# The 17 remaining contraction rows of the first MLP layer: one bf16 product over slots of split values in place of an f32 product

## The reference

```
ada = silu(c) @ W_ada + b_ada
shift_msa, scale_msa, gate_msa, shift_mlp, scale_mlp, gate_mlp = split(ada, 6)
h = layernorm(x) * (1.0 + scale_msa) + shift_msa
x = x + gate_msa * attention(h, W_qkv, b_qkv, W_proj, b_proj)
h = layernorm(x) * (1.0 + scale_mlp) + shift_mlp          # 128 x 144 per sequence
mlp = gelu(h @ W_fc1 + b_fc1, approximate=True) @ W_fc2 + b_fc2   # W_fc1 is 144 x 576
x = x + gate_mlp * mlp
# then: U = qr(P), R = expm(A(silu(cond) @ W.T + b))
x_rot = x + (z @ R - z) @ U.T,   z = x @ U                 # z is 128 x 64
```

## Time and profile before

| what | value |
|---|---|
| median of 3 runs | 407.22 us (405.56 to 407.91) |
| span of the profiled execution (first to last instruction) | 404.8 us |
| PE busy | 370.0 us, 91% |
| DVE, ACT, POOL busy | 254.6, 195.5, 134.7 us |
| chain that ended last, by engine | PE 79%, DVE 9%, ACT 4%, issue 4% |
| L1283 and L1284 | 160 instructions each, 33.3 and 30.9 us busy |
| mean granted TensorE clock | 0.959 |

### The profile page before, as it was taken

How to read it: one execution, slowest core, us unless ns; L and a number is a source line. 1 busy time by engine, 2 the same in 40 slices (tenths; PEclk the granted TensorE clock), 3 DMA queues, 4 the chain that set the end, 5 groups by cost and what they waited for, 6 DMA issues and landing times.

```text
span 404.8 us, 13218 instructions
## 1 busy us (share of the span) xinstructions
PE 370.0 (91%) x4399; PEld 289.4 (71%) x4399; DVE 254.6 (63%) x1056; ACT 195.5 (48%) x432; POOL 134.7 (33%) x400
## 2 busy tenths in 40 slices
PE   0699898889999999999999999998799999999995
PEld 0553686658777777777777777787578878787783
DVE  7560064888788789789789778968824332333233
ACT  1314444466577568568667666854233222212220
POOL 4431051543553554455455455433331000000000
PEclk9989566899999999999999999999999999999998
DMA  8515000000000000000000000000000000000000
GB/s 224 166 33 204 2 2 2 1 2 4 1 2 0 0 0 0 0 0 0 0 0 0 0 2 3 2 2 2 2 4 2 2 15 13 11 15 15 15 8 29
DMA packets 8517, 7.93 MB, mean 20 GB/s; under 512 B 1054, under 2 KB 8065, under 8 KB 8356
## 3 DMA queue, kind: packets, MB, share of 16 engines
q1 hardware_dynamic: 7776, 6.67, 5.6%
q10 hardware_dynamic: 708, 0.83, 0.7%
HBM read 6.29 MB, written 1.20 MB: 19 GB/s over the span
## 4 chain that ended last, share of the span: by engine, by line
PE 79%; DVE 9%; issue 4%; ACT 4%; DMA 1%; POOL 1%; ACTq 1%; DVEq 0%; POOLq 0%
PE bank L1283 6%; PE bank L1284 4%; PE bank L1127 4%; PE bank L1111 4%; PE bank L1145 4%; PE bank L1135 4%; PE bank L1291 4%; PE bank L1082 4%; PE bank L1100 3%; PE bank L1071 3%; PE bank L1049 3%; PE bank L1090 3%; PE bank L1072 3%; PE bank L1101 3%; PE bank L1046 2%
## 5 line engine op out<-in xcount | busy, mean ns | idle before, releaser
L423 POOL TENSOR_TENSOR root<-rec,mhalf 128x1 f32 (+1 forms) x64 | 34.6, 541 | 108.7 <-DVE Z L807 107.7
L866 DVE TENSOR_REDUCE nmax<-bank 128x4 f32<-128x512 f32 x64 | 43.2, 674 | 43.6 <-PE bank L1090 42.4
L587 ACT ACTIVATE E<-bank 128x512 f32<-128x512 f32 x64 | 38.0, 594 | 24.4 <-PE bank L1101 24.0
L609 ACT ACTIVATE gT<-bank 128x512 f32<-128x512 f32 x16 | 9.6, 597 | 65.7 <-PE bank L1284 65.7
L593 ACT ACTIVATE QT<-bank 128x512 bf16<-128x512 bf16 x32 | 19.0, 595 | 40.7 <-PE bank L1082 40.7
L597 ACT ACTIVATE KT<-bank 64x512 bf16<-64x512 bf16 x64 | 37.5, 587 | 0.8
L1100 PE MATMUL bank<-QT,KT 128*128 128x128 bf16 x256 | 36.3, 222 | 0.0
L1101 PE MATMUL bank<-NMT,headsel 128*128 128x128 bf16 x256 | 35.8, 220 | 0.0
L1135 PE MATMUL bank<-Z,sel 128*128 128x128 f32 x128 | 29.0, 310 | 6.1 <-DVE Z L813 6.1
L1283 PE MATMUL bank<-hT,wfc1a 128*128 128x128 f32 (+1 forms) x160 | 33.3, 290 | 0.0
L1100 PEld LDWEIGHTS bank<-QT,KT 128*128 128x128 bf16 x256 | 24.1, 98 | 9.7 <-issue 9.7
(11 more groups left out here) (231 smaller groups left out, 926.6 us busy)
## 6 DMA issues: line engine op xcount, KB each, us to landing
gates<-gates_dram SPq DMA_DIRECT2D x1, 2304.0 KB, 8.6
x_all<-in_x_dram SPq DMA_DIRECT2D x4, 288.0 KB, 7.5
out_dram<-x_all SPq DMA_DIRECT2D x16, 72.0 KB, 1.6
wskew<-in_L_cond_W_dram SPq DMA_DIRECT2D x4, 283.5 KB
wada<-in_L_cond_W_ada_dram ACTq DMA_DIRECT2D x1, 432.0 KB
wfc1a<-in_L_cond_W_fc_dram SPq DMA_DIRECT2D x1, 288.0 KB
wfc2a<-in_L_cond_W_fc_dram SPq DMA_DIRECT2D x1, 288.0 KB
wproj<-in_L_cond_W_proj_dram SPq DMA_DIRECT2D x16, 5.1 KB
```

What stands on the lines that cost most here:

```text
L423: link(nc.gpsimd.tensor_tensor(root[:, at], rec[:, at], mhalf[:, 0:1], ALU.pow))
L587: nc.scalar.activation(E[:, q, :, :].rearrange("p i t -> p (i t)"), bank[4][:, :], ACT.Exp).then_inc(s_E, 1)
L866: nc.vector.tensor_reduce(nmax[:, q % 2, 4 * (q // 2):4 * (q // 2) + 4], bank[3][:, :].rearrange("p (i m) -> p i m", i=4), AX.X, ALU.max, ...
```

## The change

The second product of each chunk is done in bf16, with all parts of the f32 values. Eight slots of 16 rows make up the 128 contraction rows. The 16 remaining rows of W_fc1 are loaded into six slots of `wfc1r`, three copies of the bias into three rows of a seventh. On DVE they are turned once into `wfc1b` (bf16), in which a slot holds the first, second or third bf16 part of the weights. The tokens' 16 remaining channels are spread over the eight slots by normalizing a broadcast of them (`xr`), and transposed. ACT modulates them twice, into `hR` (f32) and `hB` (bf16), with `mod2r`, the scale and shift spread over the slots by one product in the prologue. Then `parted` on DVE replaces the slots from row 64 on by the second part and those from row 96 on by the third. The sum over the slots is the sum of six of the nine products of parts.

```diff
         def _(sp):
             sp.wait_ge(k_pad, 2)
-            sp.dma_start(wfc1b[0:C2, :], W_fc1[C1:C, :]).then_inc(s_ldm, 16)
-            sp.dma_start(wfc1b[C2:K2, :], b_fc1.rearrange("(a n) -> a n", a=1)).then_inc(s_ldm, 16)
+            for n in WHOLE:
+                sp.dma_start(wfc1r[C2 * n:C2 * n + C2, :], W_fc1[C1:C, :]).then_inc(s_ldr, 16)
+            for n in range(3):
+                sp.dma_start(wfc1r[ONES + n:ONES + n + 1, :], b_fc1.rearrange("(a n) -> a n", a=1)).then_inc(s_ldr, 16)
...
+            def modulated_again(b):                                   # ACT, in place of modulated
+                wait(act, m_xnT, b + 1)
+                wait(act, m_fc1, b)
+                for t, m, o, row in ((hR, mod2r, 128, 0), (hB, mod2r, 128, 0), (hT1, mod1, 0, 2)):
+                    nc.scalar.activation(t[:, :], bank[0][:, o:o + 128], ACT.Identity, bias=m[:, row, bass.ds(b, 1)],
+                                         scale=m[:, row + 1, bass.ds(b, 1)]).then_inc(m_hT, 1)
...
             dve.wait_ge(k_id, N_ID)                                   # DVE, prologue, ahead of the wait for s_Gp
+            nc.vector.tensor_copy(rep[:, :, :], ident[0:C2, 0:C2]...to_broadcast([C2, 8, C2])).then_inc(s_rep, 1)
+            ...                                                       # five tensor_reduce and three small ones: slots
             dve.sem_inc(k_more, 1)
+            dve.wait_ge(s_rep, 9)
+            dve.wait_ge(s_ldr, 16 * 9)
+            nc.vector.tensor_copy(wfc1b[:, :], wfc1r[:, :]).then_inc(s_wB, 1)
+            STT(wfc1d[:, :], wfc1b[:, :], slots[:, 5:6], wfc1r[:, :], ALU.mult, ALU.add).then_inc(s_wB, 1)
+            nc.vector.tensor_copy(wfc1b[:, :], wfc1d[:, :]).then_inc(s_wB, 1)
+            STT(wfc1b[:, :], wfc1b[:, :], slots[:, 6:7], wfc1d[:, :], ALU.mult, ALU.add).then_inc(s_wB, 1)
+            dve.wait_ge(s_repP, 1)
+            TS(mod2r[:, 0, :], bank[6][:, 416:416 + B], ...)           # and one more for mod2r[:, 1, :]
...
+            def normalized_again(b):                                  # DVE, in place of normalized
+                TS(xn[:, 0:C1], xb[:, 0:C1], mean, rstd[:, bass.ds(b, 1)], ALU.subtract, ALU.mult).then_inc(m_xn, 1)
+                TS(xr[:, :, :], x_all[:, bass.ds(b, 1), C1:C].to_broadcast([128, 8, C2]), mean, ...).then_inc(m_xn, 1)
+
+            def parted(b):
+                wait(dve, m_hT, 3 * b + 2)
+                two, three = slice(64, 128), slice(96, 128)
+                link(TT(hD[two, :], hR[two, :], hB[two, :], ALU.subtract))
+                link(nc.vector.tensor_copy(hB[two, :], hD[two, :]))
+                TT(hB[three, :], hD[three, :], hB[three, :], ALU.subtract).then_inc(m_hB, 1)
...
             def mlp(b, parity):                                       # DVE, behind the add of b-3, ahead of xT1
+                if within(b, -1, B - 2):
+                    parted(b + 1)
...
+            def transposed_again(b):                                  # PE, in place of transposed
+                pe.transpose(bank[0][:, 128:256], xr[:, :, :]..., ident[:, :])
+                pe.transpose(bank[0][:, 0:128], xn[:, 0:C1], ident[:, :]).then_inc(m_xnT, 1)
...
-            generator_entries(0, 3)                                   # PE, prologue
+            generator_entries(0, 1)
+            pe.wait_ge(s_mod, 4)
+            pe.wait_ge(s_gsb, 1)
+            pe.wait_ge(s_rep, 1)
+            mm(bank[6][:, 416:416 + 2 * B], rep..., mod2[:, 2:4, :]..., start=True, stop=True).then_inc(s_repP, 1)
+            generator_entries(1, 3)
...
             def fc1(b):
-                wait(pe, m_hT, 2 * b + 2)
+                wait(pe, m_hT, 3 * b + 3)
                 for k in range(FK + 1):
                     mm(dst, wfc1a[:, 128 * k:128 * k + n], hT1[:, :], start=True, stop=False)
-                    ins = mm(dst, wfc1b[:, 128 * k:128 * k + n], hT2[:, :], start=False, stop=True)
+                    if k == 0:
+                        wait(pe, m_hB, b + 1)
+                    ins = mm(dst, wfc1b[:, 128 * k:128 * k + n], hB[:, :], start=False, stop=True)
```

More of the change, by code:

```diff
@@ L106, in adaln_block_then_rotation @@
         wqkv1, wqkv2 = sb("wqkv1", [C1, 3 * C]), sb("wqkv2", [128, 3 * C])
-        wfc1a, wfc1b = sb("wfc1a", [C1, FF]), sb("wfc1b", [128, FF])
+        wfc1a, wfc1b = sb("wfc1a", [C1, FF]), sb("wfc1b", [128, FF], BF16)
+        wfc1r, wfc1d = sb("wfc1r", [128, FF]), sb("wfc1d", [128, FF])
         wfc2a, wfc2b = sb("wfc2a", [128, FK, C]), sb("wfc2b", [FR + 1, C])
@@ L143, in adaln_block_then_rotation @@
         hT1, hT2 = sb("hT1", [C1, 128]), sb("hT2", [128, 128])
+        xr, hR, hD = sb("xr", [128, 8, C2]), sb("hR", [128, 128]), sb("hD", [128, 128])
+        hB = sb("hB", [128, 128], BF16)
+        rep, mod2r, slots = sb("rep", [C2, 8, C2]), sb("mod2r", [128, 2, B]), sb("slots", [128, 8])
         qk32 = sb("qk32", [128, 2, C])
@@ L222, in adaln_block_then_rotation @@
                              "s_on", "s_proj", "s_x1", "s_st1"))
+        s_rep, s_repP, s_mod2r, s_ldr, s_wB, m_hB = (sem(n) for n in ("s_rep", "s_repP", "s_mod2r", "s_ldr", "s_wB", "m_hB"))
         s_zm, s_sel, s_Grow, s_Gstep, s_root, s_Brow, s_Bstep, s_O, s_sums, s_rsum, s_div, s_pr = (
@@ L231, in adaln_block_then_rotation @@
                              "m_zT", "m_rot", "m_out"))
+        WHOLE, MIDDLE, ONES = (0, 1, 2, 4, 5, 6), (16, 80, 32), 48
         def slot(h):
@@ L366, in _ @@
             make(nc.gpsimd.memset(wqkv2[:, :], 0.0), k_pad)
-            make(nc.gpsimd.memset(wfc1b[:, :], 0.0), k_pad)
+            make(nc.gpsimd.memset(wfc1r[:, :], 0.0), k_pad)
             diagonal(ident[:, :])
@@ L565, in attention @@
                 if only(b, B + 1):
-                    modulated(0, m_xnT, m_hT, m_fc1, 0, 2, bank[0])
+                    act.wait_ge(s_mod2r, 2)
+                    modulated_again(0)
                 if prepares(b):
@@ L616, in mlp @@
                 if within(b, 0, B - 2):
[L617 removed]
+                    modulated_again(b + 1)
             lk.paired(mlp, 0, *MLP)
@@ L668, in _ @@
             dve.wait_ge(k_id, N_ID)
+            nc.vector.tensor_copy(rep[:, :, :], ident[0:C2, 0:C2].rearrange("p (a n) -> p a n", a=1)
+                                  .to_broadcast([C2, 8, C2])).then_inc(s_rep, 1)
+            for n, at in enumerate(MIDDLE):
+                nc.vector.tensor_reduce(slots[:, n:n + 1], ident[:, at:at + C2], AX.X, ALU.add).then_inc(s_rep, 1)
+            nc.vector.tensor_reduce(slots[:, 3:4], ident[:, ONES + 1:ONES + 3], AX.X, ALU.add).then_inc(s_rep, 1)
+            nc.vector.tensor_reduce(slots[:, 4:5], ident[:, ONES:ONES + C2], AX.X, ALU.add).then_inc(s_rep, 1)
+            dve.wait_ge(s_rep, 6)
+            nc.vector.tensor_reduce(slots[:, 5:6], slots[:, 0:4], AX.X, ALU.add, negate=True).then_inc(s_rep, 1)
+            STT(slots[:, 6:7], slots[:, 2:3], -1.0, ident[:, ONES + 2:ONES + 3], ALU.mult, ALU.subtract).then_inc(s_rep, 1)
+            TS(slots[:, 7:8], slots[:, 4:5], -1.0, 1.0, ALU.mult, ALU.add).then_inc(s_rep, 1)
             dve.wait_ge(s_Gp, 1)
@@ L705, in _ @@
             dve.sem_inc(k_more, 1)
+            dve.wait_ge(s_rep, 9)
+            dve.wait_ge(s_ldr, 16 * 9)
+            nc.vector.tensor_copy(wfc1b[:, :], wfc1r[:, :]).then_inc(s_wB, 1)
+            dve.wait_ge(s_wB, 1)
+            STT(wfc1d[:, :], wfc1b[:, :], slots[:, 5:6], wfc1r[:, :], ALU.mult, ALU.add).then_inc(s_wB, 1)
+            dve.wait_ge(s_wB, 2)
+            nc.vector.tensor_copy(wfc1b[:, :], wfc1d[:, :]).then_inc(s_wB, 1)
+            dve.wait_ge(s_wB, 3)
+            STT(wfc1b[:, :], wfc1b[:, :], slots[:, 6:7], wfc1d[:, :], ALU.mult, ALU.add).then_inc(s_wB, 1)
+            dve.wait_ge(s_repP, 1)
+            TS(mod2r[:, 0, :], bank[6][:, 416:416 + B], slots[:, 7:8], slots[:, 4:5], ALU.mult, ALU.add).then_inc(s_mod2r, 1)
+            TS(mod2r[:, 1, :], bank[6][:, 416 + B:416 + 2 * B], slots[:, 7:8], None, ALU.mult).then_inc(s_mod2r, 1)
             def triangles():
@@ L780, in normalized @@
                    ALU.subtract, ALU.mult).then_inc(done, 1)
+            def normalized_again(b):
+                wait(dve, m_xnT, b)
+                xb = x_all[:, bass.ds(b, 1), :].rearrange("p a c -> p (a c)")
+                mean = mv[:, bass.ds(b, 1), 0:1].rearrange("p a c -> p (a c)")
+                TS(xn[:, 0:C1], xb[:, 0:C1], mean, rstd[:, bass.ds(b, 1)], ALU.subtract, ALU.mult).then_inc(m_xn, 1)
+                TS(xr[:, :, :], x_all[:, bass.ds(b, 1), C1:C].to_broadcast([128, 8, C2]), mean, rstd[:, bass.ds(b, 1)],
+                   ALU.subtract, ALU.mult).then_inc(m_xn, 1)
+            def parted(b):
[4 more added lines that the diff above has]
+                TT(hB[three, :], hD[three, :], hB[three, :], ALU.subtract).then_inc(m_hB, 1)
             def eliminations(k, G, B):
@@ L957, in mlp @@
                 if within(b, -1, B - 3):
-                    normalized(b + 2, m_xnT, m_xn)
-            lk.paired(mlp, 1, *MLP)
```

(20 more changed lines are left out.)

4 lines of the change are left out of this document (2 added, 2 removed).

## The result

The changed kernel takes 412.75 us (median of 4 runs, 411.38 to 414.14), the kernel before 407.57 us beside it (4 runs). The ratio is 1.0141, 95% interval 1.0085 to 1.0197: slower, clear of the noise, by less than 2%. Forecast were 409.0 us; the median lies inside the stated range (406.0 to 413.0), at its upper end, and the loss is nearly three times the 1.8 us forecast. The profiled span went from 404.8 to 410.6 us. (In the changed kernel 1.75 us lie between the span and the time of the profiled run, 410.6 and 412.35; before it was 2.4. So the spans differ by 5.8 us and the medians by 5.2.)

The account below looks back on a forecast made before the run. PE was taken as the bound, 5.69 us a step. Prologue +0.35, up to fc1(3) +1.30, steps +0.03, +0.7 and +0.03, last step -0.62: +1.8, span 406.6, time 409.0 us; 8 in 10 within 406.0 to 413.0.

Parts of the forecast that it names:

- The start of the MLP stage: From fc1(0) to fc1(3): hB(0) comes late because parted(0) stands behind DVE's last variance; fc1(3) starts 1.30 us late.
- The clock: Rival: granted clock falls in the MLP stage as PE waits 0.6 of 5.7 us; up to 5 us; chance 0.05.
- slow splits: Rival: on DVE, a cast of 0.46 us or links that wait make `parted` slower; +2.6 us, 411.6; chance 0.20.
- a prologue that isn't covered: Rival: prologue conversions wait for their loads or small reductions delay Z; 2 us exposed give 411; chance 0.08.
- the low end of `parted`: Sum of the low ends of the three DVE instructions, given as 0.61 us; the step would then last 5.39.
- fc1: On PE in each step: bf16 second products shorten it from 2.56 to 1.94 us, a gain of 0.62 us.
- `parted`: On DVE ahead of xT1: three dependent instructions take 0.90 us, from 0.61 to 1.16; xT1 waits for the third.
- The steps: MLP steps: PE's gain becomes a wait for xT2; 5.72 us outside the loop, 5.76 in it, losing 0.03 and 0.07.
- The last step: Step b = 15 has no `parted`, so PE keeps its gain: -0.62 us.
- The prologue: Before the MLP: conversions on DVE hidden, first xn done at 31.1; the inserted PE product costs 0.35 us.

Follow-up runs that it names:

- the second experiment: Changed kernel with the wait for hB(0) at the first fc1 kept but filled with nine f32 products into an unused bank: 410.81 us, ratio 1.0073.
- xT first: Changed kernel with parted(b + 1) moved on DVE from ahead of the copies xT1 and xT2 to behind them: 403.73 us, ratio 0.9915.
- the kernel with the first parts earlier: Changed kernel with parted(0) moved on DVE to right behind the rotation matrices, ahead of the last variances: 407.04 us, ratio 0.9997.
- the kernel before with the wait: Kernel before, all f32, with three linked DVE instructions on scratch data added, for which fc1(0) waits behind its first product: 414.23 us, ratio 1.0179.

## Why the prediction was wrong

The step that failed is "The start of the MLP stage". It saw the wait at fc1(0) (1.90 us long, as forecast) and priced it at its own length: fc1(3) late by 1.30 us. With the clock held, the second experiment measured 17.75 us from fc1(0) to fc1(3), 1.32 more than the 16.43 before, so that sum was right. What was missing is 5.92 us: this wait lets the granted clock fall to 1.2 GHz, and what follows it, fc1(0), products(0) (the sixteen products with the rotation matrices) and fc1(1), runs at half speed. The clock stood among the rivals with a chance of 0.05, but for the waits of 0.6 us in the steps, and "up to 5 us". The place with the longest wait of the stage, which the text itself had worked out, wasn't weighed for it. The error of the whole, 4.0 us in the span (410.6 against 406.6), is that term less some smaller ones: 0.8 us up to fc1(0) and 1.1 us in the steps. That the median still lies in the range of 406.0 to 413.0 is luck: its upper part was there mostly for slow splits and a prologue that isn't covered, and neither came about. Two roundings in the sums, of 0.01 and 0.02 us (the low end of `parted` is 0.60, and fc1(0) ends 1.27 us late by its own numbers), change nothing.

The Trainium skill (TensorE: Matmul & The Clock Gate, HAM oscillation) says that waits between bursts of products put the engine back to its lower clock, and that the products behind them then run at half speed. The traces agree: 5.92 us beside the wait in the changed kernel, and 7.8 us with the wait's own 1.9 us in the kernel before. The waits for DMAs that the page shows are longer than this one; here 1.90 us were enough.

Point by point:

- **fc1.** 1.94 us forecast, 1.89 measured (357.05 to 358.94), with the dearer f32 product behind bf16 as read from the attention stage. Right. The bf16 product of 128 columns takes 0.06 us. The 81 ns that the Trainium skill (TensorE: Matmul & The Clock Gate, Back-to-back issue gap) gives for a pair of load and product in a stream don't agree with it.
- **`parted`.** 0.90 us forecast, 0.90 measured (360.54 to 361.44): 0.29, 0.22 and 0.29 us and the gaps. xT1 did start only behind the third. Its lines in the timeline of DVE, at a step outside the loop:

```profile
326.46 0.29 DVE L836 TENSOR_TENSOR hD<-hR,hB 64x128 f32<-64x128 f32 x1 [1.89 <-ACT hB L543]
326.78 0.22 DVE L837 CAST hB<-hD 64x128 bf16<-64x128 f32 x1
327.04 0.29 DVE L838 TENSOR_TENSOR hB<-hD,hB 32x128 bf16<-32x128 f32 x1
327.36 0.29 DVE L1003 COPY xT<-bank 128x128 f32<-128x128 f32 x1
327.57 0.27 DVE L1004 COPY xT<-bank 16x128 f32<-16x128 f32 x1
```

- **The steps.** 5.72 us outside the loop and 5.76 in it forecast, 5.63 and 5.67 measured (in the loop 5.63 and 5.71 by turns). The mechanism, PE's gain turned into a wait for xT2, was right and is shown by xT first. The sizes were 0.09 us too large, 1.1 us over twelve steps: fc1 was 0.05 us shorter, the rest lies in small gaps. From step 3 to step 14 the change saves 0.33 us where a loss of 0.8 was forecast.
- **The last step.** -0.62 forecast, -0.66 measured.
- **The prologue.** The inserted product cost 0.56 us, at a granted clock of 0.50, for 0.35 forecast:

```profile
29.50 0.56 PE bank L1326 x2
```

The conversions took 0.46, 0.82, 0.46 and 0.82 us and were hidden: xn was done at 31.08, as forecast (31.1). Up to the first fc1 the run was 0.44 us shorter all the same; that start differs by up to 2.8 us between profiles whatever was changed, so neither sign says anything of the edit.

Still open: why the clock fell in the steps of the profiled run of the kernel with the filled wait, and in none of the ten runs of the kernel with the first parts earlier, whose steps have the same waits; and why one of the four runs of the kernel before with the wait shows a mean clock of 0.954.

## What to carry to other kernels

Where a change makes PE wait in a stage in which it didn't, price the wait twice: by its length, and by the clock that may fall behind it; here the second was three times the first (5.92 and 1.9 us). Where an engine in front saves time, read what stands in its neighbour's program between the data and the copy that it waits for: the same three instructions behind that copy turned 1.4% slower into 2.4% faster, together with the one early `parted`. A wait that can't be removed can be filled with products into an unused bank. With no other waits behind it that gave 5.8 us; with the waits left in the steps the clock fell later in the one profile taken, and less was won (a ratio of 1.0073 in place of 1.0141).

## What the runs showed of the hardware

A wait of 1.8 to 1.9 us after a long stretch at full clock was followed by work at a granted clock of 0.50 in each of the three profiles that had it unfilled at the start of the MLP: from 307.4 to 318 us in the changed kernel, from 308 to 321 in the kernel before with the wait, from 308.8 to 319 with xT first. Some 1.7 us of work ahead of it stood another wait, of 0.63 us, but that one is in the kernel before and in the kernel with the first parts earlier too, and there the clock stayed at 1.00. Filling the long wait with products of 2.01 us in all kept the clock over it in both profiles that have them (in one it fell 15 us later). At full clock an f32 product of 128x128 with 128 columns costs 0.22 us behind f32 and 0.28 behind bf16, a bf16 one 0.06 behind either; at half clock these are 0.43, 0.53 and 0.11 us.
